# Batch 0's logits made in the attention's last waits, a new order in the expert stage's first part, and the last loads in order of use

## The reference, cut to what matters

```python
h = _layernorm(x, axis=-1) * (1 + ca) + sa
x = x + ga * _L1_attn_ref(h, slope, w_qkv, w_gate, w_out, norm_w)
h = _layernorm(x, axis=-1) * (1 + cb) + sb
x = x + gb * _L1_ffn_ref(h, gate_w, w1, w2, sw1, sw2, sw3)
# inside _L1_ffn_ref, tokens flattened:
logits = jnp.einsum('th,eh->te', x, gate_w)
scores = jax.nn.softmax(logits, axis=-1)
topk_w, topk_idx = lax.top_k(scores, TOP_K)           # TOP_K = 2
topk_w = topk_w / (topk_w.sum(-1, keepdims=True) + 1e-20)
# each expert: silu(x @ w1g) * (x @ w1u) @ w2, weighted and added;
# shared expert: the same with sw1, sw2, sw3, for all tokens
```

## Time and profile before

| what | us |
|---|---|
| median of three runs | 1146.43 |
| profiled execution, and its span from first to last instruction | 1145.18, 1143.5 |
| TensorE busy, share of the span | 1060.2, 93% |
| VectorE, ScalarE, GpSimd busy | 895.2, 736.2, 334.6 |
| last instruction of the attention stage (VectorE L1313 ends) | 964.14 |
| first instruction of the expert stage | 965.43 |
| VectorE: eight memsets, then means (L2255) start | 965.51, 965.71 |
| TensorE: squares (L1673), logits of batch 0 (L1678) | 1.84, 1.55 |
| GpSimd: one sum of squares (L1970), median | 1.31 |
| 32 scatters of rows, first start to last end | 971.98 to 1021.34 |
| loop of tiles on TensorE | about 1026 to 1116 |
| loads of results issued from | 1119.83 |
| one tile of the loop | 2.12 |

### The profile page before, as it was taken

One profiled execution on the slowest core, in us unless ns is written; L12 is line 12 of the kernel. 1 busy time (PEld: TensorE's weight loads), 2 busy tenths in 40 slices (PEclk: granted clock), 3 DMA queues, 4 the chain that ended last, 5 costly groups with the idle time before them and its releaser, 6 DMA issues. The chain is left out here.

```text
span 1143.5 us, 22333 instructions
## 1 busy us (share of the span) xinstructions
PE 1060.2 (93%) x7536; PEld 923.7 (81%) x7536; DVE 895.2 (78%) x1817; ACT 736.2 (64%) x1399; POOL 334.6 (29%) x335
## 2 busy tenths in 40 slices
PE   5888888879999999999999999999999997979996
PEld 4656666658899899899898898898998986769994
DVE  5788988857788788788788788788788787867775
ACT  4679797767766666666666666666666654625661
POOL 3353544442311201211111111111111234753440
PEclk9889999979999999999999999999999998989999
DMA  7210001010401311311311211221221291824436
GB/s 256 94 52 16 16 6 44 14 50 23 137 21 50 112 47 47 108 45 52 100 51 53 94 58 53 89 62 53 80 71 54 83 45 66 355 98 116 123 98 234
DMA packets 67881, 92.13 MB, mean 81 GB/s; under 512 B 22658, under 2 KB 46338, under 8 KB 66787
## 3 DMA queue, kind: packets, MB, share of 16 engines
q1 hardware_dynamic: 64402, 81.83, 24.6%
q0 software_dynamic: 3408, 9.39, 2.2%
HBM read 46.35 MB, written 42.75 MB: 78 GB/s over the span
## 5 line engine op out<-in xcount | busy, mean ns | idle before, releaser
L1551 PE MATMUL all_psum<-all_h_parts,attn_wp 128*128 128x512 f32 x1140 | 297.6, 396 | 0.0
L1551 PEld LDWEIGHTS all_psum<-all_h_parts,attn_wp 128*128 128x128 f32 x1140 | 209.8, 189 | 39.7
L1723 ACT CAST attn_pp<-attn_p 128x512 fp32r<-128x512 f32 (+3 forms) x256 | 117.4, 459 | 187.8 <-DVE attn_p L1831 185.7
L1812 DVE TENSOR_TENSOR attn_pp<-attn_p,attn_pp 128x512 fp32r<-128x512 f32 (+3 forms) x256 | 198.0, 773 | 6.5 <-ACT attn_pp L1723 6.5
L1970 POOL TENSOR_TENSOR all_gate<-all_gate,attn_sq 128x512 f32<-128x512 f32 x64 | 84.7, 1324 | 369.8 <-ACT attn_sq L1734 369.7
L1630 PE MATMUL all_psum<-attn_qkp 128*128 128x512 f32 (+3 forms) x768 | 164.9, 323 | 3.7 <-DVE attn_qkp L1812 3.7
L1577 PE MATMUL all_psum<-attn_pp,attn_vp 128*128 128x512 f32 (+3 forms) x768 | 163.8, 322 | 1.0 <-DVE attn_pp L1812 0.5
L1577 PEld LDWEIGHTS all_psum<-attn_pp,attn_vp 128*128 128x128 f32 x768 | 129.4, 189 | 21.6 <-issue 1.2
L1630 PEld LDWEIGHTS all_psum<-attn_qkp 128*128 128x128 f32 x768 | 124.8, 190 | 12.6 <-issue 4.3
L1831 DVE TENSOR_TENSOR attn_p<-all_psum,attn_mask 128x512 f32<-128x512 f32 (+3 forms) x256 | 123.5, 482 | 2.1 <-PE all_psum L1630 0.9
L1054 DVE TENSOR_REDUCE front_top<-all_psum 128x2 f32<-128x256 f32 (+3 forms) x128 | 99.4, 815 | 17.8 <-PE all_psum L695 16.8
(11 more groups left out here) (381 smaller groups left out, 1899.5 us busy)
## 6 DMA issues: line engine op xcount, KB each, us to landing
expert_rows<-attn_empty SPq DMA_DIRECT2D x8, 2080.0 KB, 12.7
expert_weight_parts<-all_wraw SPq DMA_DIRECT2D x32, 304.0 KB, 2.4
experts_wx<-expert_weight_parts SPq DMA_DIRECT2D x8, 1216.0 KB, 16.6
all_wraw<-in_w1p SPq DMA_DIRECT2D x8, 1024.0 KB, 5.9
all_yacc<-expert_rows SPq DMA_DIRECT2D x39, 130.5 KB
all_wraw<-in_wx SPq DMA_DIRECT2D x16, 304.0 KB, 3.0
attn_mask<-decay_masks SPq DMA_DIRECT2D x16, 256.0 KB, 2.6
all_x<-in_x SPq DMA_DIRECT2D x4, 512.0 KB, 7.0
```

The source lines that it names most:

```text
L1551: last = nc.tensor.matmul(out, wp[:, a, k, col:col + P], hh[:, c, k, b * S:(b + 1) * S], start=(m == 0), stop=(m == 5))
L1723: nc.scalar.copy(pp[:, u % 2, 0, cols], p[:, cols]).then_inc(p_hi, 1)
L1812: nc.vector.tensor_tensor(out, whole, high.bitcast(F32), ALU.subtract).then_inc(ready, 1)
```

## The change

It has three parts.

1. Batch 0's logits. The router weights are loaded at the start of the attention stage, their high part is made by ScalarE in unit 5 of the first pair and their low part by GpSimd in unit 6. Batch 0's low part is made by GpSimd behind `pool_update` of batch 1. TensorE makes the logits between the last values and the last outputs, ScalarE copies them out behind its last unit, TensorE turns them into bank 1 from column 64 on, ahead of the squares. The expert stage begins with `choose(0)` reading that bank.
2. The expert stage's first part is written in another order on TensorE, ScalarE and VectorE. GpSimd's order stays.
3. The results' last batch is loaded in two parts rather than one, and loads, additions and stores go in one order: tiles 0-1, 2-3, 12-13, 14-15, 4-7, 8-9, 10-11. Before, loads went 0-1, 12-15, 2-3, 4-7, 8-9, 10-11, and additions and stores 0-1, 2-3, 4-7, 12-13, 14-15, 8-9, 10-11.

```diff
-    def vector_low(self, nc, dve, n, b):
-        dve.wait_ge(self.high_done, n + 1)
+    def pool_low(self, nc, pool, n, b):
+        pool.wait_ge(self.high_done, n + 1)
...
-        nc.vector.tensor_tensor(hp[:, 1, :, cols], self.ht[:, :, :], hp[:, 0, :, cols].bitcast(F32),
+        nc.gpsimd.tensor_tensor(hp[:, 1, :, cols], self.ht[:, :, :], hp[:, 0, :, cols].bitcast(F32),
                                 ALU.subtract).then_inc(self.low_done, 1)
...  # TensorE, attention's end
                 for j in range(NB):
                     values(j, UNITS - 1, PAIRS - 1)
+                pe.wait_ge(late_norm.low_done, 1)
+                pe.wait_ge(rw_low, 1)
+                for m, (k, (a, c)) in enumerate([(k, tc) for k in range(KT) for tc in TERMS]):
+                    last = nc.tensor.matmul(ps[0:E, LOGITS_BANK, :], t["rwp"][:, a, k, :], hh[:, c, k, 0:S],
+                                            start=(m == 0), stop=(m == 5))
+                last.then_inc(routed, 1)
                 pe.wait_ge(y_added, PAIRS * 2 * B - 2)
...
+                pe.wait_ge(logits_copied, 1)
+                for tt in range(TB):
+                    last = nc.tensor.transpose(ps[:, SQUARES_BANK, SCORES_AT + tt * E:SCORES_AT + (tt + 1) * E],
+                                               logits_t[:, tt * P:(tt + 1) * P], t["ident"][0:E, 0:E])
+                last.then_inc(logits_turned, 1)
                 pe.wait_ge(summed, PAIRS * UNITS)
...  # ScalarE
-                act.wait_ge(raw_loaded, 48)
-                nc.scalar.copy(t["rwp"][:, 0], t["rw"][:, :, :]).then_inc(rw_high, 1)
                 for u in (UNITS - 2, UNITS - 1):
                     finish_unit(u, PAIRS - 1)
                 act.wait_ge(routed, 1)
+                act.wait_ge(wx_stored, PAIRS * 64)
+                nc.scalar.copy(logits_t, ps[0:E, LOGITS_BANK, :]).then_inc(logits_copied, 1)
...  # VectorE
                 y_low(UNITS - 1, PAIRS - 1)
-                dve.wait_ge(rw_high, 1)
-                low(t["rwp"][:, 1], t["rw"][:, :, :], t["rwp"][:, 0], rw_low)
-                late_norm.vector_low(nc, dve, 0, 0)
                 late_norm.vector_stats(nc, dve, 1, 1)
...  # GpSimd
                         if last_pair and u == NEXT_AT + 1:
                             late_norm.pool_update(nc, pool, 1, 1)
+                            late_norm.pool_low(nc, pool, 0, 0)
...  # expert stage, ScalarE
                 nc.scalar.copy(identr[:, :], t["ident"][:, :]).then_inc(ident_ready, 1)
-                copy_logits(0)
                 shared_high(0)
...  # expert stage, the end
-        PARTS = [slice(0, 2), LAST, slice(2, TB), slice(TB, 2 * TB), slice(2 * TB, 2 * TB + 2), slice(2 * TB + 2, 3 * TB)]
+        PARTS = [slice(0, 2), slice(2, TB), LAST[0], LAST[1], slice(TB, 2 * TB), slice(2 * TB, 2 * TB + 2),
+                 slice(2 * TB + 2, 3 * TB)]
-        DONE = [PARTS[0], PARTS[2], PARTS[3], BY_TENSOR[0], BY_TENSOR[1], PARTS[4], PARTS[5]]
+        DONE = PARTS
```

110 lines of the change are left out of this document (56 added, 54 removed).

## The result

The changed kernel took 1148.78 us (median of 12 runs), the kernel before 1146.07 beside it (12 runs). The ratio is 1.0023, 95% interval 1.0014 to 1.0032: 1.6 to 3.7 us slower. Forecast were 1145.5, the range 1143.2 to 1147.9, and a chance of 0.09 for slower.

What follows compares the result with a forecast made beforehand. TensorE, busy 93%, was taken as the bound, with GpSimd's scatters setting the expert stage's end; terms 0.0 - 0.5 + 0.0 - 0.4 = -0.9 us gave 1144.3 for the profiled execution, 1145.5 as median, range 1143.2 to 1147.9.

Steps and rivals of the forecast that it cites:

- Attention's end, 0.0: End of the attention stage: two VectorE instructions less (2.3 us) offset by GpSimd's port holding; 0.0, ends -0.4 and +1.1.
- rival B: GpSimd's low part holds up VectorE at the attention's end and costs more than it gives: +1.9, 1148.3 us; chance 0.14.
- First scatter, 971.6: Expert stage's start: GpSimd's first scatter at 971.6, 0.4 us earlier, 0.3 behind the rows ready at 971.3.
- Variances and batch 1's first scatter, -0.5: Expert stage, new VectorE order: variances and power 0.5 us earlier, batch 1's first scatter near 988.2; ends -1.1 and +0.3.
- Later scatters, 0.0: Expert stage, scatters after batch 1's first: same VectorE instructions beside them in another order; 0.0, ends -1.0 and +1.0.
- No compute engine sets its end: GpSimd does.: Expert stage, 965.4 to 1026 us: its end is set by GpSimd's 32 scatters in a row, 1.27 us each.
- Loads and stores at the end, -0.4: Program's end: VectorE about 0.2 us earlier, batch 3's stores no longer behind a 6.1 us wait; -0.4, ends -0.9 and +0.3.
- Loop of tiles, 0: Loop of 39 tiles: unchanged at 2.12 us a tile; a longer or shorter loop would show the forecast wrong.

Runs made afterwards that it cites:

- e_part1: The change with the expert stage's order and the end of before, so only batch 0's logits moved; 1150.23 against 1150.32 us, ratio 1.0004.
- e_tail_only: The kernel before with only the third part of the change (last batch loaded in two parts, one order of loads, additions, stores); 1151.20 us, ratio 1.0012.
- the control: The kernel before, unchanged, run and profiled again on a later chip; ratio to before 0.9999.
- e_before_buf3: The kernel before with three buffers of outgoing rows rather than two; ratio to before 1.0008.
- e_best: The changed kernel with the old end and, from gates(3) on, the old order; 1149.07 against 1149.25 us of before, ratio 0.9999.

## Why the prediction was wrong, point by point

- *Attention's end, 0.0.* Came out -0.6, just outside its range. The holding at the port came as forecast (1.65 and 1.75 for subtractions that take 0.28 and 0.7 when free), but 0.68 of it went into a wait of VectorE that was there already, so the shift is 1.7 where 2.3 was put; rival B fell. The logits on TensorE ran at half clock (2.76) and lay in the wait but for 0.4.
- *First scatter, 971.6.* At the change's stage start it was to come 0.4 earlier and came 0.0 earlier (6.54 both). The rows were ready at 5.56 behind the stage's start (forecast 5.9), but 0.3 was put between rows and scatter where it is 0.98. Before's own rows hid this: there both distances end at the same moment (970.99 + 0.99 and 971.66 + 0.32, both 971.98).
- *Variances and batch 1's first scatter, -0.5.* Right in size: -0.6 each. But the term was put down to the new order, and most of it is part one's: `e_part1`, in the old order, has the first scatter of batch 1 at 22.87 behind the stage's start, `e_tail_only`, without part one on the same chip, at 23.25. The scatter at 976.28 was held again (3.50 us) and ended at 979.78, 0.83 after VectorE's additions. The Trainium skill, SBUF — State Buffer, "Who interferes with whom", infers that a tensor_tensor doesn't hold up descriptor generation; this row contradicts it as the one of before did.
- *Later scatters, 0.0.* The last starts 0.4 earlier counted from the stage, so 0.2 of the 0.6 are lost on the way. Within the range, and without effect.
- *"No compute engine sets its end: GpSimd does."* This is the step that failed. It was true of before, by 2.1 us of slack only, and the forecast never asked what came second: the shared experts' chain through batch 3's choice, the map, `down(4)`, `down(5)` and `output(2)`, for which the loop waits. The prediction gave the order behind batch 1's slots no term but the scatters'. In the pair of profiles on the first chip that chain comes 3.7 later: 1.8 by `token_rows(2, 1)` behind `down(1)` (`lower(2)` waits 1.75), 1.2 by `turn_logits(3)` behind `gates(3)` and `ups(3)`, 0.9 between choice and map, 0.3 between map and `down(4)`, and 0.5 less behind it, where the down matmuls ran partly at full clock. Less the slack of 2.1 the loop starts 1.5 later, where -0.5 was forecast. That parts two and three cost is shown by runs; this division is read from one pair of profiles, and on the later chips, where stops lie in the same stretch, the loop starts only 0.5 later than in the control.
- *Loads and stores at the end, -0.4.* Wrong in sign: +0.9 here, about +1.1 over the profiles (median 21.7 of seven with the new end against 20.7 of eight with the old, from the late down matmuls on). VectorE now makes the last batch's products and additions (1131.95 to 1135.08) ahead of the product that the x sums need, so TensorE idles longer, at 3.90, and the clock falls. The forecast took 1.98 for the sums from the earlier trace rows and didn't ask whether a longer wait changes them.
- *Loop of tiles, 0.* -0.8 here; over the profiles 92.2 to 94.4 in no relation to the order. Not explained.

Terms of the pair: +2.1 (start, no part of the change), -0.6, +1.5, -0.8, +0.9: 3.1. The medians differ by 2.7. What can be laid to the change is -0.6 + 1.5 + 0.9 = 1.8, which lies inside the interval (1.6 to 3.7); for the other 0.9 of the medians' difference no stretch of the profiles can be named.

## What to carry to other kernels

When one chain sets the end of a stage, write down the second one and its slack before moving anything: here 2.1 us of slack were spent, and more, by two short pieces of TensorE's work (the last rows of batch 2 and the turned logits of batch 3) that moved behind longer ones while ScalarE and VectorE waited for them. The move that catches the eye, `output(1)` behind three instructions, cost 0.2 or 0.3. A reordering has to be walked through for every instruction that another engine waits for, not only for those near the wait that is to go. And a change that lengthens TensorE's wait ahead of a short run of matmuls has to price these at half clock (3.4 to 3.8 us instead of 1.98), or fill the wait, and no longer than it lasts (here 1.1 us too long).

## What the runs showed that was not expected

- GpSimd's first scatter waits for VectorE's slots and ScalarE's rows. In all 17 profiles it starts at the later of two sums, slots plus 0.30 to 0.33 us and rows plus 0.98 to 0.99. Why the second is 0.7 longer is open.
- The same program takes 1146 us on one chip and 1149 to 1151 on four others. In three profiles there (the control, `e_before_buf3`, `e_tail_only`) VectorE stops twice, for 2.9 and 5.5 to 5.6 us, and ScalarE with it; a third buffer didn't change it. In other orders the stops have other lengths, and in `e_best` the second isn't seen, yet batch 3's ranks come no more than 0.6 earlier. The cause is open.
- Six added matmuls of 512 columns, whose result nobody reads, shortened the x sums from 3.78 to 1.88 us and the end from 23.2 (21.2 in another profile of this end on the chip) to 20.9, though they delayed the x sums by 1.1.
